# High half of the probabilities by a second exponential from PSUM, in the two local-attention layers

## What is computed

```python
q, k, v = split(shift_token(x) @ wqkv)            # 8 heads of 64
q, k = rotary_xpos(l2norm(q) * qs, l2norm(k) * ksc)
sim = einsum('bhwid,bhwjd->bhwij', bq * 8.0, look_around(k))   # windows of 128, own and previous
attn = softmax(where(mask, -max, sim), axis=-1)
x = x + merge(einsum('bhwij,bhwjd->bhwid', attn, look_around(v))) @ wo
h = layernorm(shift_token(x)) * lg + lb
a, g = split(h @ w1 + b1)
x = x + (a * gelu(g)) @ w2 + b2
```

## Time and profile before

| | |
|---|---|
| median of 3 runs | 3927.06 us (3926.61 to 3927.91) |
| the profiled execution | 3927.97 us, its span 3926.1 us |
| mean granted PE clock | 0.953 of full speed |
| exponentials at line 1245 | 256 of 128x896 |
| copies to the high part, line 1253 | 256 |
| subtractions for the low part, line 1374 | 256 |

### The profile page before, as it was taken

How to read it: one execution, slowest core, us unless ns; L and a number is a source line. 1 busy time by engine, 2 the same in 40 slices (tenths; PEclk the granted TensorE clock), 3 DMA queues, 4 the chain that set the end, 5 groups by cost and what they waited for, 6 DMA issues and landing times.

```text
span 3926.1 us, 77200 instructions
## 1 busy us (share of the span) xinstructions
PE 3360.0 (86%) x29600; PEld 1960.8 (50%) x29600; DVE 2846.7 (73%) x4121; ACT 2352.7 (60%) x2813; POOL 1511.6 (39%) x1171
## 2 busy tenths in 40 slices
PE   2888888888855799998999989878999899998998
PEld 1223232323223566565666666545656666665665
DVE  4778787777745777777777776667877777777764
ACT  0566666565643566666656666555666666666654
POOL 1212121212104445455444554443545544455443
PEclk7999999999987899999999999988999999999999
DMA  2222222222211000000000001010010100101000
GB/s 56 49 61 54 60 53 60 52 60 52 51 50 39 15 20 19 27 19 29 19 20 26 25 23 36 30 44 24 25 32 24 35 29 24 32 29 36 24 27 30
DMA packets 149008, 139.11 MB, mean 35 GB/s; under 512 B 11132, under 2 KB 147376, under 8 KB 148912
## 3 DMA queue, kind: packets, MB, share of 16 engines
q1 hardware_dynamic: 148912, 137.78, 13.4%
HBM read 70.40 MB, written 33.55 MB: 26 GB/s over the span
## 4 chain that ended last, share of the span: by engine, by line
PE 35%; DVE 15%; ACT 11%; issue 7%; POOL 1%; DMA 1%; SPq 0%; DVEq 0%; ACTq 0%; POOLq 0%
PE f_p L1026 13%; PE f_p L1162 7%; DVE f_Ph L1374 6%; PE f_p L1133 5%; PE f_p L1052 3%; PE f_p L1043 3%; ACT f_Ph L1253 2%; ACT f_Pl L1245 2%; DVE f_xh L1456 2%; PE f_p L1059 2%; ACT f_hT L1274 1%; DVE f_rt L248 1%; ACT f_gates L1268 1%; DVE f_xT_l L1343 1%; PE f_p L1008 1%
## 5 line engine op out<-in xcount | busy, mean ns | idle before, releaser
L654 DVE TENSOR_REDUCE m_negm<-m_p 128x2 f16<-128x1024 f32 x512 | 608.7, 1222 | 169.2 <-PE m_p L473 167.5
L576 ACT ACTIVATE m_Pr<-m_p 128x1024 f32<-128x1024 f32 x512 | 500.4, 1020 | 164.0 <-PE m_p L492 159.6
L1374 DVE TENSOR_TENSOR f_Ph<-f_Pl,f_Ph 128x896 f16<-128x896 f32 x256 | 377.0, 1514 | 213.3 <-ACT f_Ph L1253 213.3
L1540 POOL TENSOR_TENSOR f_u<-f_u,f_bt 128x1024 f32<-128x1024 f32 x128 | 301.8, 2358 | 465.6 <-DVE f_bt L1359 465.6
L1556 POOL TENSOR_TENSOR f_hT<-f_gates,f_hT 128x512 f16<-128x512 f32 x192 | 234.2, 1223 | 587.9 <-ACT f_gates L1276 587.6
L1268 ACT ACTIVATE f_gates<-f_p,f_bias 128x512 f32<-128x512 f32 x192 | 131.4, 684 | 469.0 <-PE f_p L1162 469.0
L501 PE MATMUL m_o<-m_Pr,m_vm 128*32 128x512 f32 x2048 | 341.6, 646 | 13.0 <-ACT m_Pr L576 13.0
L1026 PE MATMUL f_p<-f_wq_h,f_xT_h 128*128 128x512 f16 x768 | 307.0, 400 | 26.1 <-DVE f_xhT_l L1462 12.7
L1545 POOL TENSOR_TENSOR f_u<-f_u,f_rn 128x1024 f32<-128x1024 f32 x128 | 289.1, 2258 | 74.3 <-DVE f_mark_v L1387 74.3
L1392 DVE TENSOR_REDUCE f_negm<-f_p 128x4 bf16<-128x1024 f32 x256 | 300.8, 1222 | 17.0 <-PE f_p L1059 16.6
L1026 PE MATMUL f_p<-f_wq_l,f_xT_h 128*128 128x512 f16 x768 | 305.3, 398 | 0.0
(11 more groups left out here) (235 smaller groups left out, 8540.8 us busy)
## 6 DMA issues: line engine op xcount, KB each, us to landing
f_xs<-out SPq DMA_DIRECT2D x32, 512.0 KB, 4.4
f_xr<-out SPq DMA_DIRECT2D x32, 512.0 KB, 5.0
out<-f_xb SPq DMA_DIRECT2D x32, 512.0 KB, 3.0
m_xin<-in_L_attn_x SPq DMA_DIRECT2D x16, 512.0 KB, 4.1
out<-m_xn SPq DMA_DIRECT2D x16, 512.0 KB, 3.0
m_QT<-m_hi SPq DMA_DIRECT2D x128, 64.0 KB
m_KT<-m_hi SPq DMA_DIRECT2D x128, 64.0 KB
m_xr<-in_L_attn_x SPq DMA_DIRECT2D x16, 512.0 KB, 4.7
```

What stands on the lines that cost most here:

```text
L576: act.activation(Pr[kt % 2][:, 2 * u:2 * u + 2, :].rearrange("p h t -> p (h t)"), psum[w.slot("M2", g, kt, u)][:, :], ACT.Exp).then_inc(*w ...
L654: dve.tensor_reduce(negm[:, t, pr // 2, :, pr % 2], psum[w.slot("M1", h, u)][:, :].rearrange("p (a k) -> p a k", a=2), AX.X, ALU.max, nega ...
L1374: dve.tensor_tensor(Pp[h % 4][:, 1, :], Pl[h % 2][:], Pp[h % 4][:, 0, :], ALU.subtract).then_inc(*p_lo_ready.up(I))
L1540: pool.tensor_tensor(u[t][:], u[t][:], bt[:], ALU.add).then_inc(*bt_used.up(I))
```

## The change

The step PH and its semaphore go. In `l2` ACT takes two exponentials of each head's scores, the first to the 32-bit tile, the second straight to the 16-bit high part, and the slot of the scores is freed after the second. The wait for the PV of the pair two back now stands ahead of both exponentials of pairs 2 and 3. The low part waits for the slot's release, that is for the second exponential. The orders of PE, DVE, POOL and SP are as before.

```diff
         "ACT": """...
-               F.H1,0 F.W1,2 F.H1,1 F.W1,3 C.LM F.H1,2 F.W1,4 F.H1,3 F.W1,5 F.H1,4 F.H1,5 C.L2,0 C.PH,0 A.HI,0 C.L2,1 C.PH,1 C.L2,2
-               C.PH,2 A.HI,1 C.L2,3 C.PH,3 N.XH A.HI,2 A.HI,3""",
+               F.H1,0 F.W1,2 F.H1,1 F.W1,3 C.LM F.H1,2 F.W1,4 F.H1,3 F.W1,5 F.H1,4 F.H1,5 C.L2,0 A.HI,0 C.L2,1 C.L2,2 A.HI,1 C.L2,3 N.XH A.HI,2 A.HI,3""",
...
             def l2(I, hp):
+                if hp >= 2:
+                    act.wait_ge(*w.is_full("PV", hp - 2))
                 for h in (2 * hp, 2 * hp + 1):
                     act.wait_ge(*w.is_full("L2", h))
                     if h >= 2:
                         act.wait_ge(*p_lo_ready.at(I, h - 1))
-                    act.activation(Pl[h % 2][:], psum[w.slot("L2", h)][:, 0:NK], ACT.Exp, scale=1 / KBOOST)\
-                        .then_inc(*w.frees("L2", h))
-
-            def p_hi(I, hp):
-                if hp >= 2:
-                    act.wait_ge(*w.is_full("PV", hp - 2))
-                for h in (2 * hp, 2 * hp + 1):
-                    act.wait_ge(*w.is_drained("L2", h))
-                    act.activation(Pp[h % 4][:, 0, :], Pl[h % 2][:], ACT.Copy).then_inc(*p_hi_ready.up(I))
+                    scores = psum[w.slot("L2", h)][:, 0:NK]
+                    act.activation(Pl[h % 2][:], scores, ACT.Exp, scale=1 / KBOOST)
+                    act.activation(Pp[h % 4][:, 0, :], scores, ACT.Exp, scale=1 / KBOOST).then_inc(*w.frees("L2", h))
...
             def p_lo(I, hp):
                 for h in (2 * hp, 2 * hp + 1):
-                    dve.wait_ge(*p_hi_ready.at(I, h + 1))
+                    dve.wait_ge(*w.is_drained("L2", h))
                     dve.tensor_tensor(Pp[h % 4][:, 1, :], Pl[h % 2][:], Pp[h % 4][:, 0, :], ALU.subtract).then_inc(*p_lo_ready.up(I))
```

More of the change, by code:

```diff
@@ L945, in layers_phase @@
         q_lo_ready, hs_ready = S("q_lo_ready"), S("hs_ready")
-        p_hi_ready, p_lo_ready, v_hi_ready = S("p_hi_ready"), S("p_lo_ready"), S("v_hi_ready")
+        p_lo_ready, v_hi_ready = S("p_lo_ready"), S("v_hi_ready")
         on_ready, mv_ready, rstd_ready, rstd_link = S("on_ready"), S("mv_ready"), S("rstd_ready"), S("rstd_link")
@@ L1278, in _ @@
             w.run({"WQ": wq, "WO_": wo_weights, "WF": wf, "XT": xt, "QK": qk, "V": v_, "HI": hi, "ST": st, "LM": lm, "L2": l2,
-                   "PH": p_hi, "OT": ot, "XH": xh_, "W1": w1_, "H1": h1})
+                   "OT": ot, "XH": xh_, "W1": w1_, "H1": h1})
         @block.vector
```

## The result

The changed kernel takes 3947.25 us (median of 5 runs, 3944.82 to 3950.06) against 3927.06 us for the one before (3923.31 to 3927.91 in the same comparison): a ratio of 1.0053, interval 1.0038 to 1.0067. It is **slower by 20 us**, and outside the range of the prediction (3915 to 3939 us).

What follows compares the result with a forecast made beforehand. The prediction took the end of the eighth subtraction to set a round's length. Full rounds -2.9, tails +4.4 and other four rounds -2 summed to -0.5 us: 3927.5 us profiled, 3926.6 us median, range 3915 to 3939 us.

Steps and rivals of the forecast that it cites:

- The price of the exponential: Second exponential on ACT in place of the copy: 0.92 us each, at most 8 us less busy time, worth 0.
- Pair 1 and the turns: Heads 2 and 3: subtraction 2 goes ahead of POOL's f_klt; the fourth subtraction ends near 1926.6 instead of 1928.31.
- Slower 1: POOL's f_klt goes ahead of subtraction 2 in full rounds: +0.17 us a round, 3934 to 3938 us; chance 0.2.
- The moved wait up to L2,3's start: ACT's head 4 exponential starts at 1928.32 instead of 1926.94; L2,3 starts at 1930.15, not 1929.67.
- The end of the round, -0.11 us: Last subtraction ends at 1939.30 against 1939.41, ACT's 1.3 us delay hidden behind POOL's f_u; 26 rounds, -2.9 us.
- The tails: In both layers' tails POOL is quiet and nothing hides the wait: +1.65 and +2.74 us, +4.4 us together.
- The other four rounds: "Second" rounds level; in each "third" round one subtraction less meets POOL, -1 us each: -2 us.
- The clock: Low-clock stretches in full rounds may shift, 0.3 us a round, -7 or +7 us; no new one expected; gain chance 0.12.
- Slower 2: ACT becomes the path at the last subtraction, head 7 1.26 us later: up to 33 us, 3940 to 3960; chance 0.08.
- Theory 3: Set up for the experiments: the price of the second exponential, or the slot it holds, is the cost; no size.
- Theory 2: Set up for the experiments: the moved wait itself delays ACT, whatever the clock; at most 0.8 us each for heads 4, 6.
- theory 1: Set up for the experiments: PE's longer pause before L2,3 brings low clock there, 4.1 us instead of 2.5 us.

Runs made afterwards that it cites:

- run 4: Kernel before the change, with only the wait for PV moved ahead of the first exponentials of pairs 2 and 3, copy kept: 3938.12 us, 1.0029.
- run 3: Changed kernel plus 6 idle matmuls of 512 columns on PE ahead of L2,3 (the small filler): 3937.25 us, 1.0023.
- run 1: Changed kernel with the wait for PV put between the first and second exponential of heads 4 and 6: 3894.99 us, 0.9918; repeated, 3896.37 us, 0.9921.
- run 5: Kernel before the change, with the copy replaced by a second exponential from PSUM that frees the slot, order and waits kept: 3934.97 us, 1.0017.
- runs 6 and 7: On run 1's kernel: 6 idle matmuls ahead of PV,3, 3886.63 us; second exponential turned back into a copy, 3904.08 us, with those matmuls 3897.03 us.

## Why the prediction was wrong

Its steps, one by one:

- **The price of the exponential**: 0.92 us on average for one of line 1248 (0.91 to 0.97) against my 0.92. Right, and worth nothing by itself.
- **Pair 1 and the turns**: right. Subtraction 3 ended 9.74 into the round (predicted 9.8), with f_klt waiting for subtraction 2, in every full round. Slower 1 did not come about. That was close: f_klt asked 0.01 us later.
- **The moved wait up to L2,3's start**: right (11.50 and 13.37 us, predicted 11.48 and 13.31).
- **The end of the round, -0.11 us**: right where L2,3 is fast. In the first round of layer 1 head 6's exponential started at 17.39 (predicted 17.32), the evacuations began at 22.38 against 22.50 before, and the round took 80.48 us. L2,3 is fast in 3 of 26 rounds only.
- **The tails**: nearly right. The last subtraction came 1.96 and 2.69 us later into the tail (predicted 1.65 and 2.74). These rows are the last subtraction in the tails of layers 1 and 2, against the earlier trace rows:

```profile
2506.05 1.09 DVE L1369 TENSOR_TENSOR f_Ph<-f_Pl,f_Ph 128x896 f16<-128x896 f32 x1 [0.53 <-ACT f_Ph L1248]
...
3873.68 1.09 DVE L1369 TENSOR_TENSOR f_Ph<-f_Pl,f_Ph 128x896 f16<-128x896 f32 x1 [0.53 <-ACT f_Ph L1248]
```

- **The other four rounds**: 0.3 us longer in all, not 2 shorter. The two "third" rounds were 0.7 and 0.4 us shorter (I had 1 each), but "second" of layer 2 was 2.2 us longer, with a slow L2,3 in it (3.87 us). A small miss.
- **The clock: this step failed.** I wrote "the pause before PV,3 gets shorter, so I see no new low stretch", one sentence after I had noted that the pause before L2,3 gets longer. I weighed one pause and not the other. I also took 3.91 us from L2,3's start to PV,1's end out of a round in which L2,3 was fast and carried it over as a constant. With L2,3 at 1.2 GHz this term is 5.5 us, so ACT's heads 6 and 7 come 1.7 us later than I reckoned. My slack at subtraction 7 was 0.7 us; what goes beyond it counts, 0.91 us against before in a slow round.
- **What I left out.** I let the end of the eighth subtraction alone set the length of a round, and did not follow the late exponentials on to ACT's high parts for row tiles 2 and 3. In a slow round these are 1.5 us late, and by way of POOL and the evacuation of v they set the round's length: 1.49 us more than a round of before without a low stretch, not 0.91.

The Trainium skill, TensorE: Matmul & The Clock Gate, section "A second HAM failure mode: psum-queue depth-cycling", tells of a kernel in which PE idles briefly between groups of matmuls as the PSUM slots go round, and loses its clock again and again. The trace agrees: a slot held 0.8 us longer, a pause 0.5 us longer, and a granted clock of 0.58 behind it. In the tails it does not: the pause there is 1.91 us, and L2,3 runs at full speed. My prediction named another section of the same page and gave its rule too little weight.

How the 20 us add up, as far as the runs show it, in the profiled executions (22.0 us apart, 2.2 of them ahead of the layers):

- 15.5 us lie in the 26 full rounds. With the small filler, which takes the low clock off L2,3, the same rounds are 1.2 us longer than before. So some 14 us (11 with the repetition of the changed kernel) come with the low clock on L2,3, given that the moved wait has used up ACT's slack. The filler costs 3.2 us of that in the other four rounds and 1.0 in the tails, which is why the kernel gains 10 us by it (3947.4 against 3937.3) and not more.
- 4.0 us are the two tails with what follows them; the wait alone (run 4) makes them 3.8 us longer.
- 0.3 us are the other four rounds.
- The 1.2 us that remain with the filler, although the last subtraction is 0.12 us earlier than before, are by the windows of run 3 (0.98 and 0.96 against 0.98 and 1.00 in the earlier trace rows) again the clock, later in the round.

These are differences between single executions.

**Slower 2** named the right place (ACT late at subtraction 7) and the right band, 3940 to 3960 us, but it did not name the clock as what uses up the slack, and had a chance of 0.08. No theory stands as the sole cause. Theory 3 falls by run 1. Theory 2 falls by run 3, which keeps the wait and is 10 us faster; run 4, the wait with no slow L2,3, costs the other 10. And theory 1 alone falls by layer 1 of run 5, where slow L2,3 steps without the moved wait cost next to nothing.

**What stays open.** Whether the length of the pause alone decides, or its place against the rest of the round: the first full round of layer 1, the first two of layer 2 and, in the repetition, the last three of layer 2 have the pause of 1.98 us and no slow L2,3; the tails have none behind 1.91 us; and "third" rounds before had a slow one behind 1.32 us. Nor do the runs say why the pauses of the two layers differ by 0.1 us in run 5, or why its layer 2 has two low stretches a round. None of this was tried.

## What to carry to other kernels

Where an edit holds a PSUM slot longer, look up how long PE already pauses for it, and reckon the round a second time with the step behind the pause at the low clock; if the slack does not bear that, the change is not free. Put a wait directly ahead of the instruction that needs it, not ahead of its group: here that one line was worth 51 us (3947.4 to 3896.4 on one chip). A few idle matmuls in a pause that cannot be removed can pay, but count what the loop body grows by. And when a step is late, follow every step queued behind it on its engine to the end of the round, not only the one that waits for it first.

## What the runs showed of the hardware

- A low stretch on L2,3 came with a longer pause ahead of it: in no full round at 1.48 us or less, in 5 of 13 at 1.75 us, 13 of 13 at 1.87 us, 23 and 20 of 26 at 1.98 us. The pause is not the whole rule, as the exceptions above show.
- It drifts: in the middle of layer 1 after, L2,3 took 4.07 us, and seven rounds later 3.50, as the stretch began later against the round (0.5 us behind L2,3's start in the one, 1.2 in the other) and lay more on PV,1. Head 6's exponential moved by 0.1 us only (19.01 to 18.91), and the rounds kept a length of 81.8 to 81.9 us.
- Six idle matmuls a round made a kernel faster three times: by 10 us ahead of L2,3, by 8 to 10 and by 7 us ahead of PV,3 (runs 6 and 7).
- With eighteen more matmuls in the loop body one execution had stops of 3.7 to 4.4 us in ten of 13 full rounds of one layer and none in the other, with 157 packets in the instruction queue instead of 66. With six more there was no such stop (67 packets).
